# Loading and splitting Wq, Wg and Wo of an eight-core attention and expert kernel in another place and by other queues

## What is computed

```python
q = elu(split_heads(x @ Wq + bq)) + 1.0
k = elu(split_heads(x @ Wk + bk)) + 1.0
v = split_heads(x @ Wv + bv)
kv = einsum('bhsd,bhse->bhde', k, v)
attn = merge_heads(einsum('bhsd,bhde->bhse', q, kv))
gate = sigmoid(x @ Wg + bg)
x = layernorm(x + (gate * attn) @ Wo + bo)
x = layernorm(x + experts(x) + shared_expert(x))
```

## Time and profile before

| what | value |
|---|---|
| runs shown | 6691.61 and 7621.22 us, their median 7156.41 us |
| the profiled execution | 6698.0 us |
| span of its slowest core (core 4) | 6696.5 us, granted clock 0.923 |
| spans of the eight cores | 6685.7 to 6696.5 us |
| busy in that span | PE 5705.6 us (85%), DVE 1731.6, ACT 688.3, POOL 1140.7 |
| first loop, between, second loop (core 4) | PE ends the first loop at about 602.8 us and starts the second at 744.2; the second ends near 1590 |

### The profile page before, as it was taken

How to read it: one execution, slowest core, us unless ns; L and a number is a source line. 1 busy time by engine, 2 the same in 40 slices (tenths; PEclk the granted TensorE clock), 3 DMA queues, 4 the chain that set the end, 5 groups by cost and what they waited for, 6 DMA issues and landing times.

```text
span 6696.5 us, 66786 instructions; the slowest of 8 cores (6685.7 to 6696.5 us)
## 1 busy us (share of the span) xinstructions
PE 5705.6 (85%) x27750; PEld 2740.8 (41%) x27750; DVE 1731.6 (26%) x2464; ACT 688.3 (10%) x1126; POOL 1140.7 (17%) x612
## 2 busy tenths in 40 slices
PE   3884477874999999999999595899999999999686
PEld 1442364552444444444444242344444444444232
DVE  2221133332222222222222013222223222222113
ACT  1111122221000000000000001000000000000001
POOL 0001111011321221222120200321122122111110
PEclk9897687886999999999999797999999999999898
DMA  2001101002422222222221213432222222221211
GB/s 70 19 16 41 54 35 38 20 32 84 111 76 59 80 81 64 70 79 78 60 80 35 76 28 96 112 85 73 66 79 82 57 77 78 72 66 52 62 43 51
DMA packets 149088, 425.00 MB, mean 63 GB/s; under 512 B 11155, under 2 KB 11427, under 8 KB 148662
## 3 DMA queue, kind: packets, MB, share of 16 engines
q1 hardware_dynamic: 106102, 271.82, 12.1%
q0 software_dynamic: 40384, 140.53, 9.7%
q10 hardware_dynamic: 2304, 8.39, 0.4%
HBM read 282.28 MB, written 25.17 MB: 46 GB/s over the span
## 4 chain that ended last, share of the span: by engine, by line
PE 79%; DMA 7%; DVE 6%; POOL 3%; ACT 2%; issue 2%; DVEq 0%; SPq 0%; ACTq 0%; POOLq 0%
PE pb L240 26%; PE pb L242 26%; PE pb L243 25%; DMA PW<-PW 2%; DMA PW<-ws 2%; POOL PW L1000 1%; DVE PM L958 1%; PE pb L882 1%; DMA PS<-h_scr 1%; DMA PW<-w 1%; POOL PW L734 1%; POOL PW L400 1%; DVE PM L965 1%; DVE PA L556 0%; ACT PA L560 0%
## 5 line engine op out<-in xcount | busy, mean ns | idle before, releaser
L240 PE MATMUL pb<-PA,PW 128*128 128x512 bf16 (+1 forms) x5632 | 2039.3, 362 | 188.1 <-POOL PW L1000 154.6
L242 PE MATMUL pb<-PA,PW 128*128 128x512 bf16 (+1 forms) x5632 | 2038.9, 362 | 0.0
L243 PE MATMUL pb<-PA,PW 128*128 128x512 bf16 (+1 forms) x5632 | 2037.7, 362 | 0.0
L240 PE MATMUL pb<-PW,PM 128*128 128x512 bf16 x2304 | 892.0, 387 | 111.0 <-DVE PM L965 63.5
L734 POOL TENSOR_TENSOR PW<-PW 128x2048 bf16<-128x2048 f32 x192 | 784.8, 4088 | 739.1 <-DMA PW<-PW 739.1
L242 PE MATMUL pb<-PW,PM 128*128 128x512 bf16 x2304 | 892.1, 387 | 0.0
L243 PE MATMUL pb<-PW,PM 128*128 128x512 bf16 x2304 | 891.2, 387 | 0.0
L240 PEld LDWEIGHTS pb<-PA,PW 128*128 128x128 bf16 x5632 | 554.6, 98 | 777.3 <-issue 227.0
L953 DVE TENSOR_TENSOR PM<-pb,PM 128x512 f32<-128x512 f32 x256 | 177.0, 692 | 2500.1 <-PE pb L243 2500.1
L243 PEld LDWEIGHTS pb<-PA,PW 128*128 128x128 bf16 x5632 | 554.8, 99 | 562.4 <-issue 7.9
L242 PEld LDWEIGHTS pb<-PA,PW 128*128 128x128 bf16 x5632 | 554.3, 98 | 556.8 <-issue 6.5
(11 more groups left out here) (147 smaller groups left out, 2406.1 us busy)
## 6 DMA issues: line engine op xcount, KB each, us to landing
PW<-w SPq DMA_DIRECT2D x192, 1024.0 KB, 5.2
PW<-PW POOLq DMA_DIRECT2D x216, 512.0 KB, 4.1
PW<-ws SPq DMA_DIRECT2D x24, 1024.0 KB, 5.0
PA<-x SPq DMA_DIRECT2D x28, 512.0 KB, 3.6
h_scr<-PA POOLq DMA_DIRECT2D x16, 512.0 KB, 2.9
PS<-h_scr ACTq DMA_DIRECT2D x16, 512.0 KB, 3.3
out<-PM POOLq DMA_DIRECT2D x16, 512.0 KB, 2.9
PW<-Wk SPq DMA_DIRECT2D x4, 1024.0 KB, 5.2
```

The costliest lines, as they stand in the source:

```text
L240: Sd.pe(lambda e: e.matmul(bk_ap, sh, mh, start=first, stop=False), waits=waits0, want=False)
L242: Sd.pe(lambda e: e.matmul(bk_ap, sh, ml, start=False, stop=False), want=False)
L243: return Sd.pe(lambda e: e.matmul(bk_ap, sl, mh, start=False, stop=last), want=want)
```

## The change

Three things are done.

1. Wq moves into the first loop. Wo and Wq swap their places in `PW`, so that Wq lands in columns 16384 to 24575, which the first loop does not use. After tiles 6, 8, 10 and 12, one quarter each is loaded by a DMA in ACT's list, its hi part copied by ACT, its lo part computed by POOL.
2. Wg and Wo stay between the loops, but through two stages: Wg through `wstage`, loaded by DMAs in ACT's list, and Wo through `stage2` (columns of `PM` with the biases of k and v, no longer needed), loaded by SP. The quarters of the two alternate in POOL's list. The hi parts are written by converting DMAs of POOL, not by ACT.
3. POOL's four loads of x now stand ahead of these, and the first write into the columns of `stage2` in the expert part waits for the last of Wo.

```diff
+        wq_hi = PW[:, 16384:20480].bitcast(BF16)
+        wq_lo = PW[:, 20480:24576].bitcast(BF16)
...
+        wo_hi = PW[:, 0:4096].bitcast(BF16)
+        wo_lo = PW[:, 4096:8192].bitcast(BF16)
+        wq_chain = stage_free
...
             kk_guard = kv_last
 
+            if t in (6, 8, 10, 12):
+                half = (t - 6) // 2
+                ev_l = Sd.dma("se", lambda e, half=half: e.dma_start(
+                    out=wstage.rearrange("p (c i) -> p c i", c=2),
+                    in_=wq_h[half * 256:(half + 1) * 256].rearrange("(c p) i -> p c i", p=128)),
+                    waits=[wq_chain], inc="WB")
...
+                ev_hi = Sd.se(lambda e, hi_ap=hi_ap: e.copy(out=hi_ap, in_=wstage),
+                              waits=[ev_l])
+                ev_lo = Sd.add("gp", lambda e, hi_ap=hi_ap, lo_ap=lo_ap: e.tensor_tensor(
+                    out=lo_ap, in0=wstage, in1=hi_ap, op=ALU.subtract),
+                    waits=[ev_hi], inc="GP")
+                wq_chain = ev_lo
+                wb_ev[0][half] = ev_lo
...
-        for wi, hbm in ((0, wq_h), (1, wg_h), (2, wo_h)):
...
-                ev_l = Sd.dma("sy", lambda e, hbm=hbm, half=half: e.dma_start(
...
-                ev_hi = Sd.se(lambda e, hi_ap=hi_ap: e.copy(out=hi_ap, in_=wstage),
-                              waits=[ev_l, barA_pe] if (wi == 0 and half == 0) else [ev_l])
-                ev_lo = Sd.add("gp", lambda e, hi_ap=hi_ap, lo_ap=lo_ap: e.tensor_tensor(
...
+        stage2 = PM[:, 144:2192]
+        wg_chain = wq_chain
+        wo_chain = None
+        for half in range(4):
+            ev_l = Sd.dma("se", lambda e, half=half: e.dma_start(
...
+                waits=[wg_chain], inc="WB")
...
+            ev_hi = Sd.dma("gp", lambda e, hi_ap=hi_ap: e.dma_start(
+                out=hi_ap, in_=wstage),
+                waits=[ev_l, barA_pe] if half == 0 else [ev_l], inc="GPD")
+            ev_lo = Sd.add("gp", lambda e, hi_ap=hi_ap, lo_ap=lo_ap: e.tensor_tensor(
+                out=lo_ap, in0=wstage, in1=hi_ap, op=ALU.subtract),
+                waits=[ev_hi], inc="GP")
+            wg_chain = ev_lo
...
+            ev_l2 = Sd.dma("sy", lambda e, half=half: e.dma_start(
...
+                waits=(list(barA) if half == 0 else [wo_chain]), inc="WB2")
...
+            ev_hi2 = Sd.dma("gp", lambda e, hi_ap2=hi_ap2: e.dma_start(
+                out=hi_ap2, in_=stage2),
+                waits=[ev_l2, barA_pe] if half == 0 else [ev_l2], inc="GPD")
+            ev_lo2 = Sd.add("gp", lambda e, hi_ap2=hi_ap2, lo_ap2=lo_ap2: e.tensor_tensor(
+                out=lo_ap2, in0=stage2, in1=hi_ap2, op=ALU.subtract),
+                waits=[ev_hi2], inc="GP")
+            wo_chain = ev_lo2
...
-                        waits=[cb_mm[hf]])
+                        waits=[cb_mm[hf], stage2_guard])
```

More of the change, by code:

```diff
@@ L237, in build_program @@
                 wa_ev[wi][half] = ev_lo
+        wq_hi = PW[:, 16384:20480].bitcast(BF16)
+        wq_lo = PW[:, 20480:24576].bitcast(BF16)
+        wg_hi = PW[:, 8192:12288].bitcast(BF16)
+        wg_lo = PW[:, 12288:16384].bitcast(BF16)
+        wo_hi = PW[:, 0:4096].bitcast(BF16)
+        wo_lo = PW[:, 4096:8192].bitcast(BF16)
+        wb_ev = [[None] * 4, [None] * 4, [None] * 4]
+        wq_chain = stage_free
         def mm3s(bk_ap, sh, sl, mh, ml, first, last, waits0, want=True):
@@ L358, in build_program @@
             kk_guard = kv_last
+            if t in (6, 8, 10, 12):
[4 more added lines that the diff above has]
+                    waits=[wq_chain], inc="WB")
+                hi_ap = wq_hi[:, half * 2048:(half + 1) * 2048]
+                lo_ap = wq_lo[:, half * 2048:(half + 1) * 2048]
+                ev_hi = Sd.se(lambda e, hi_ap=hi_ap: e.copy(out=hi_ap, in_=wstage),
[5 more added lines that the diff above has]
+                wb_ev[0][half] = ev_lo
         a_ve_tail = ("VE", Sd.cnt["VE"])
@@ L441, in build_program @@
             xb_pre[cc0] = ev
+        stage2 = PM[:, 144:2192]
[3 more added lines that the diff above has]
+            ev_l = Sd.dma("se", lambda e, half=half: e.dma_start(
+                out=wstage.rearrange("p (c i) -> p c i", c=2),
+                in_=wg_h[half * 256:(half + 1) * 256].rearrange("(c p) i -> p c i", p=128)),
+                waits=[wg_chain], inc="WB")
+            hi_ap = wg_hi[:, half * 2048:(half + 1) * 2048]
+            lo_ap = wg_lo[:, half * 2048:(half + 1) * 2048]
+            ev_hi = Sd.dma("gp", lambda e, hi_ap=hi_ap: e.dma_start(
[5 more added lines that the diff above has]
+            wg_chain = ev_lo
+            wb_ev[1][half] = ev_lo
+            ev_l2 = Sd.dma("sy", lambda e, half=half: e.dma_start(
+                out=stage2.rearrange("p (c i) -> p c i", c=2),
+                in_=wo_h[half * 256:(half + 1) * 256].rearrange("(c p) i -> p c i", p=128)),
+                waits=(list(barA) if half == 0 else [wo_chain]), inc="WB2")
+            hi_ap2 = wo_hi[:, half * 2048:(half + 1) * 2048]
+            lo_ap2 = wo_lo[:, half * 2048:(half + 1) * 2048]
+            ev_hi2 = Sd.dma("gp", lambda e, hi_ap2=hi_ap2: e.dma_start(
[5 more added lines that the diff above has]
+            wo_chain = ev_lo2
+            wb_ev[2][half] = ev_lo2
+        stage_free_b = [wg_chain]
+        stage2_guard = wo_chain
         xTb_cons = None
```

25 lines of the change are left out of this document (2 added, 23 removed).

## The result

Against the kernel before, the changed kernel takes 0.993 of its time, 95% interval 0.991 to 0.995: 47 us less, 31 to 63. In many executions of either kernel the cores of one die or of both had a lower granted clock, which puts the medians of all runs at 7074 us (changed) and 7313 us (before); without that the changed kernel takes 6643.6 to 6647.4 us and the one before 6690.6 to 6698, and from here on every number is from cores without it.

The account below looks back on a forecast made before the run. The one-stage weight rounds between the loops, holding ACT's list and so PE (idle 141.5 us), were taken as the bound this change could touch. Terms -86 + 12 + 4 = -70 us from 6698.0 gave 6628 us, range 6600 to 6664.

Parts of the forecast that it names:

- What bounds: Between the loops: PE idle 141.5 us behind twelve one-stage rounds of 11.15 us and ACT's list; at most 137.3 us winnable.
- The time: Whole kernel: 6698 less 70 gives 6628 us, range 6600 to 6664; 0.96 for within 2% of before.
- First loop, +12: After tiles 6, 8, 10, 12: ACT makes hi of x 3.0 us late, four times, 12 us; bounds 6 to 24.
- Between the loops, -86: ACT held for five POOL rounds of 8.4 us plus 1.0 contention in four; first hi of x 85.9 us earlier.
- a crowded pair: Converting DMA and subtraction with other transfers under way: subtraction 5.99 us after issue instead of 4.28, taken as 1.7 more.
- the rule at its end: Between the loops: each converting DMA waits for most of a load, 3 us in four rounds; sum 8 us higher.
- Subtractions meeting VectorE, +4: Second loop's start, steps for q: two of three POOL subtractions delay PE 2.2 us each, 4 us; bounds 0 and 7.
- Weights late next: Gate and product with Wo: last quarters of Wg and Wo arrive in time, by 11 and 34 us.
- the first: Rival between the loops: waiting DMAs do not hold ACT, the gate waits for Wg instead; 6610 us, chance 0.04.
- The second, crowding: Rival between the loops: converting DMAs take 14.0 us beside loads, five rounds of 18.1; 6673 us, chance 0.08.
- The clock: Rival in the first loop: TensorE stays at 1.2 GHz for tiles 7 to 14, 136 us more; 6764 us, chance 0.02.

Follow-up runs that it names:

- Order alone: Changed kernel with the first loop's copy and subtraction of Wq placed behind the next tile's hi of x; mean span 6630.0 us against 6630.2 (cores 4 to 7).
- the variant with staggered loads: Changed kernel, each load but each matrix's first also waiting for the converting DMA issued with it to land; hold 62.5 us, mean span 6626.3 us against 6630.5.
- the three-stage version: Changed kernel with three stages, ACT's hi copies, SP's loads, Wg's first two quarters loaded early, copies of Wq, Wg, Wo placed later; 6565.0 to 6570.9 us.
- the last version: Three-stage version with lo of kv behind the first chunk's four lo of x and Wo's first two quarters exchanging stages; 6557 to 6561 us, 0.979 of before.

## Why the prediction was right or wrong

**What bounds.** Right. The stretch was the loads and splits between the loops, and ACT's list was the one that held the second loop in the changed kernel, by the fourth issue of a Wg load: the experiment that moved the issues to SP let it go, and the hold fell from 66 to 2.7 us.

**The time.** The forecast of 6628 us, a gain of 70, stands against 6643.8 us and a gain of 54 in the profiled executions, and 47 (31 to 63) by the ratio. The executions of 6643.6 to 6647.4 us lie in the range of 6600 to 6664; the median of all runs, 7074 us, lies far outside it. The prediction set the forecast beside 6692 to 6698 us and not beside the median of 7156, and no term of it allowed for a median: as a number for the median of all runs it was wrong. The gain was overstated by a third to a half, by the terms below; that the kernel would stay within 2% of before was right.

**First loop, +12.** The place was right, and the size was too on the cores that kept tiles 30.8 us apart (13 us on cores 3 and 7), but that is in part luck. ACT's delay was mis-sized: hi of x came 1.6 us late and not 3.0 (6.82 us behind hi of v, 5.23 the tile before), since ACT's list issued the load at the start of hi of v (327.63) and not behind it, and the first product came 1.3 us late. TensorE's clock, for which the central sum took nothing beyond the 6.0 slow us of the tile shown, made up the rest of the 3.3 us per quarter: 1.0 in the products and 0.9 in the next gap. The tile of the earlier trace rows was not the usual one either: its spacing is 32.4 us. Order alone took 10.3 us of it back. The mean over the cores, +6.7, is smaller: on cores 0 to 2 the tiles ahead of the first held gap happened to be 28.4 and 29.7 us apart, and on cores 4 to 6 a tile of 28.4 came in later. The prediction had no term for that; the spread is one reason why the slowest core gained less than the mean.

**Between the loops, -86.** This is the step that failed, in its term for contention: "I take 1.0 for each of four rounds, bounds 0 and 1.7". From one issue to the next the four took 12.4 to 13.1 us on core 3 and 12.0 to 12.3 in the mean on each of the others, instead of 8.4, since a converting DMA took 8.2 to 9.0 us beside a load and 4.3 without one. The row that I took for a crowded pair, was none. The DMA issues of the kernel before from 2425 to 2445 us show one load:

```profile
PW<-w SPq DMA_DIRECT2D x1, 1024.0 KB, 5.3
PW<-PW POOLq DMA_DIRECT2D x1, 512.0 KB, 5.8
```

It is the load issued at 2443.98, when the converting DMA (5.8 us) had landed; nothing but a small fetch of instructions lay beside it. Why it took 5.8 us is open: the 192 converting DMAs of line 732 took 4.1 to 6.4 us. Core 4 of before had no load beside a converting DMA at all, so the bound of 1.7 us stood on nothing. The sentence on the Trainium skill ("DMA: Bandwidth & Descriptors", "Issuing engines are not separate DMA queues") pointed the right way; the rule at its end, about 3 us a round, was nearer than my 1.0, and the runs show still more. The first load was also counted at 5.1 and landed after 6.9 on core 3 (8.6 in the mean of the cores, 12.0 at most), with loads of x and Wo beside it. Together the hold was 66.0 us (66.8 on core 3) instead of 51.4. The loads themselves were free, as said, since each ended inside the other matrix's round.

**Subtractions meeting VectorE, +4.** Right in mechanism, place and number of hits (two), 6.5 us instead of 4, inside its bounds of 0 and 7. Leaving the subtractions out took exactly this away.

**Weights late next.** Right: from 690 to 800 us no wait of PE over 1 us is for POOL or a load on any core, so neither the gate nor the product with Wo waited for a weight.

The sum with the measured sizes on core 3 is -68.5 (hold 135.3 to 66.8) + 11.2 + 5.9 = -51.4, and the core's span fell by 53.0.

**The rivals.** ACT was held, so the first is out. The second, crowding, was the right mechanism at less than half of its price: 12.7 us a round on core 3, not 18. It should have had its own share of the central sum. The clock did not stay down: the products behind a held gap ran at 0.90 and those of the next tile at 0.94, and the spacings grew by 3.3 us for two tiles and not by 34.

## What to carry to other kernels

A second stage pays less when the transfers that fill and empty it run at the same time: here a load and a converting DMA issued together both took some 8 us, and a copy by an idle engine (1.9 us) was better. Ask what each engine's list holds behind a waiting instruction, and put work for a later stage behind the next item of the path, not ahead of it. And take most care with the order in which weights are needed: Wq's move, with the loads of x ahead, brought 44 of 57 us, and taking Wg ahead of Wo, once SP issued the loads, brought 27 (the start of the experts on cores 4 to 7, 1523.2 to 1495.8), more than the 13 of the rest of the change.

## What was not expected of the hardware

- A load of 1 MB and a converting DMA of 1 MB to 512 KB in flight together land after 8.4 and 8.2 us, against 5.1 and 4.3 alone: near to one after the other (9.4). The changed kernel's core 3 from 642 to 694 us, then two pieces of it (a load beside a converting DMA, and the subtraction behind them) and the first load beside those of x and Wo. The last two columns are the mean busy share of the 16 DMA engines and GB/s:

```profile
642.00:694.00 52.00, 0.00 (x0) 0.00 (x0) 0.00 (x0) 0.00 (x0) 19.35 (x10) 0.50 0.48 121
...
681.14:689.40 8.26, 0.00 (x0) 0.00 (x0) 0.00 (x0) 0.00 (x0) 0.56 (x2) 0.50 0.80 190
689.53:693.50 3.97, 0.00 (x0) 0.00 (x0) 0.00 (x0) 0.00 (x0) 3.97 (x1) 0.50 0.00 0
...
626.40:633.30 6.90, 1.94 (x8) 1.57 (x8) 1.22 (x1) 0.97 (x1) 0.00 (x0) 0.50 1.02 413
```

  And the variant with staggered loads on core 5, over as long a stretch as the first:

```profile
633.00:685.00 52.00, 1.94 (x8) 1.57 (x8) 1.82 (x3) 2.03 (x4) 27.07 (x11) 0.50 0.55 151
```

  The 0.48 is a mean over overlaps and subtractions: the 16 DMA engines were busy 0.67 to 0.80 of the time while a load and a converting DMA ran together (177 to 190 GB/s) and not at all during the subtractions. Staggered, the load runs under the subtraction, and the whole stretch has 151 GB/s at 0.55. Alone, a load had 0.65 (214 GB/s, 614.17 to 619.08 before) and a converting DMA 0.63, so together they filled hardly more than either alone, while loads beside loads had 1.02 and 413 GB/s. Why a converting DMA does not leave room for a load was not tried.
- A VectorE instruction with two inputs in SBUF can be held through several GpSimd subtractions that follow each other: 10.76 us, to 1.1 us behind the end of the third, on all eight cores of the three-stage version, and 7.22 us across two on core 3 of the last one. It is not always so: on core 2 of the last version it began at 613.60 within one subtraction and ended at 617.65, and the next subtraction, begun at 616.53, took 5.05 us instead of 4.06. VectorE's lo of x, with one input in PSUM, took its 0.69 us beside a subtraction (core 7, 616.87, subtraction from 616.22).
- The tiles of the first loop lock into few spacings (30.8; 32.4, 29.7, 29.9; or 28.4, 29.7), which differ by core and run and move the end of that loop by up to 20 us with the same program. They go with the granted clock from a tile's first product to its hi of v, on all cores of the kernel before: 1.00 where the spacing is 28.4 to 29.9 us, 0.93 to 0.97 where it is 30.8, 0.88 to 0.90 where it is 32.4. On core 0 of the changed kernel it was 1.00 up to the first held gap and 0.92 to 0.96 behind it. What moves a core from one pattern to another was not tried.
